# The part in front of the tile loop rebuilt in a kernel with patch attention and two window-attention layers

## What is computed

```
xn = layernorm(x)                        # x: (1, 2048, 128), float32
# patch attention on xn
qkv  = xn[:, patch_index, :] @ Wqkv.T    # 26 patches of 20 rows
attn = softmax(q @ k.T * 8**-0.5)        # 16 heads
p    = xn.at[:, patch_index, :].set(attn @ v) @ Wout.T + bout
# two layers, f = xn at first
h = shift_token(f)                       # the upper 64 channels one position later
q, k, v = split(h @ wqkv)                # q, k: normalised per head, scaled, rotated
f = f + local_attention(q, k, v) @ wo
h = layernorm(shift_token(f)); a, g = split(h @ w1 + b1)
f = f + (a * gelu(g)) @ w2 + b2
out = x + p + f
```

## Time and profile before

| what | us |
|---|---|
| median of 3 runs | 424.98 |
| lowest and highest run | 422.65, 426.35 |
| the profiled execution, whole | 424.36 |
| span of that execution, first to last instruction | 422.2 |
| PE busy in the span | 364.5 |
| DVE busy | 293.7 |
| ACT busy | 297.3 |
| POOL busy | 257.5 |

### The profile page before, as it was taken

The page is one execution under the profiler, slowest core; times in us unless marked ns, Lnnn a source line. Parts: engine busy times, 40 slices in busy tenths (PEclk is TensorE's granted clock), DMA queues, the critical chain, the costliest instruction groups (busy, mean ns, idle before and its releaser), DMA issues. The chain is left out here.

```text
span 422.2 us, 10798 instructions
## 1 busy us (share of the span) xinstructions
PE 364.5 (86%) x3999; PEld 277.9 (66%) x3999; DVE 293.7 (70%) x525; ACT 297.3 (70%) x909; POOL 257.5 (61%) x232
## 2 busy tenths in 40 slices
PE   1737855799999999998969878799999999988995
PEld 0626644578888888876636446688888888765563
DVE  4797875587787777864745766678777787565363
ACT  2334651689999898998617468889989899974621
POOL 2173589598888888892003548988888888710000
PEclk9976995899999999999989989999999999999999
DMA  8920000123232232231320003123223222110001
GB/s 294 347 77 2 2 2 2 37 53 74 50 73 61 57 71 53 63 71 33 92 121 0 0 0 77 44 55 71 57 57 73 51 68 66 46 36 12 25 25 50
DMA packets 34514, 25.80 MB, mean 61 GB/s; under 512 B 18933, under 2 KB 29087, under 8 KB 33951
## 3 DMA queue, kind: packets, MB, share of 16 engines
q1 hardware_dynamic: 34175, 24.66, 21.8%
q10 hardware_dynamic: 288, 0.46, 0.4%
HBM read 9.64 MB, written 1.05 MB: 25 GB/s over the span
## 5 line engine op out<-in xcount | busy, mean ns | idle before, releaser
L1006 ACT ACTIVATE probs<-ps,neg_max 128x128 f32<-128x128 f32 x256 | 90.1, 378 | 5.5 <-DVE neg_max L1229 4.4
L531 POOL TENSOR_TENSOR qkn<-rot 128x512 f32<-128x512 f32 x64 | 80.5, 1280 | 11.7 <-PE ps L728 4.1
L539 POOL TENSOR_TENSOR qkn<-qkn,rnorm 128x512 f32<-128x512 f32 x64 | 65.5, 1045 | 22.9 <-ACT rnorm L956 22.9
L545 POOL TENSOR_TENSOR probs_n<-probs,row_inv 128x512 f32<-128x512 f32 x64 | 66.6, 1042 | 19.1 <-DVE row_inv L1234 16.2
L1006 ACT ACTIVATION_READ_ACCUMULATOR probs<-ps,neg_max 128x1 f32 x256 | 55.4, 216 | 0.0
L949 ACT ACTIVATE sq<-ps 128x1024 f32<-128x1024 f32 x32 | 32.8, 1026 | 30.0 <-DVE rot L1181 19.2
L520 POOL TENSOR_TENSOR h_lo<-xin,h_hi 64x512 fp32r<-64x512 f32 x16 | 20.6, 1290 | 43.1 <-DVE sin_w L1189 26.9
L1229 DVE TENSOR_REDUCE neg_max<-ps 128x4 f32<-128x512 f32 x64 | 41.0, 681 | 8.3 <-PE ps L742 8.3
L173 PE MATMUL ps<-wqkv_hi,h_hi 128*128 128x512 f32 x96 | 42.8, 446 | 0.0
L1181 DVE TENSOR_TENSOR rot<-ps,cos_w 128x1024 f32<-128x1024 f32 x32 | 39.1, 1221 | 3.6 <-PE ps L175 3.0
L1171 DVE TENSOR_REDUCE ss<-sq 128x16 f32<-128x1024 f32 x32 | 38.8, 1212 | 3.9 <-ACT sq L949 3.8
(11 more groups left out here) (127 smaller groups left out, 806.1 us busy)
## 6 DMA issues: line engine op xcount, KB each, us to landing
v_off<-v_tok SPq DMA_DIRECT2D x64, 128.0 KB, 2.3
k_t<-k_t SPq DMA_DIRECT2D x30, 128.0 KB, 2.3
cos_w<-in_cos_t SPq DMA_DIRECT2D x2, 1024.0 KB, 7.9
sin_w<-in_sin_t SPq DMA_DIRECT2D x2, 1024.0 KB, 9.5
x_shift<-x SPq DMA_DIRECT2D x64, 32.0 KB, 1.9
x_raw<-in_x SPq DMA_DIRECT2D x4, 256.0 KB, 4.7
out<-o_t SPq DMA_DIRECT2D x4, 256.0 KB, 2.3
x_shift<-in_wqkv SPq DMA_DIRECT2D x1, 768.0 KB, 7.4
```

Source lines behind the costliest of these rows:

```text
L531: pool.tensor_tensor(to, first, second[:, :, ::-1, :], ALU.add).then_inc(rot_summed, 1)
L539: pool.tensor_tensor(of, of, rnorm[:, part * HEADS:(part + 1) * HEADS].unsqueeze(2) .broadcast_to([P, HEADS, DH]), ALU.mult).then_inc(rot_ ...
L545: pool.tensor_tensor(probs_n[:, 4 * g:4 * g + 4, :], probs[:, 4 * g:4 * g + 4, :], row_inv[:, 4 * g:4 * g + 4].unsqueeze(2).broadcast_to([ ...
L1006: e = act.activation(probs[:, k, :], s_ps[g][:, cw * P:(cw + 1) * P], ACT.Exp, bias=neg_max[:, k:k + 1], accum_out=row_sum[:, k:k + 1])
```

## The change

Most of it is in front of the loop.

- Patch projections: queries and keys for all blocks in two chunks of 272 columns straight from `xin` (`project_patch_qk`, `take_patch_qk`), in place of 112 columns per step. The staging on DVE is gone; POOL repeats the patches with six copies (`repeat_patches`), blocks 0 to 5, 6 to 11 and 12.
- Patch softmax: the unnormalised exponential is turned. The values get four columns of ones per group of heads (`A_VAL` = 36 in place of 32), so that the weighing gives the sums too, and DVE divides its output from PSUM (`patch_out`). The outputs of all steps are kept and turned at the end, four steps first and then three, and put with one strided copy each.
- Input: spans 2 and 3 are normalised at the end of DVE's steps 0 and 1, turned in PE's steps 2 and 3. The shifted input for the tile projection is made by two DMAs per span (`shift_input`) into `xs`, which lies in x1; ACT rounds it in one piece (`round_first`, steps 3 to 6), POOL splits it in one piece: spans 0 and 1 before the loop, spans 2 and 3 in the loop's steps 1 and 3.
- POOL's order before the loop: ones, repeats, tables, wqkv of layer 0, split of span 0, masks, split of span 1, w1. Layer 1's wqkv is rounded and split by POOL after the first layer's tiles; the unpatched positions are copied by a DMA on SP.
- Semaphores: cos, sin and the scales have one each. SP loads the scales and wqkv of layer 0 first, then cos, sin, masks. The masks arrive in `w_raw`, and `probs_t` has two buffers of its own.

Constants, SP and POOL:

```diff
+A_CHUNK = 272
+A_VAL = 36
+TURN_FIRST = 4
...
+            shift_input(0)
+            shift_input(1)
             sp.dma_start(wo_s[:], wo.rearrange("l (c p) n -> p l c n", p=P)).then_inc(w_in, 16)
...
+            shift_input(2)
+            shift_input(3)
             sp.wait_ge(xn_tr, SPANS)
             sp.dma_start(w1_raw, w1.rearrange("l p n -> p l n")).then_inc(w1_in, 16)
+            sp.wait_ge(masks_done, 1)
+            sp.dma_start(wqkv_raw[1], wqkv[1]).then_inc(wqkv_in[1], 16)
+            sp.wait_ge(a_ot_done, 2)
+            sp.dma_start(x_patch[:, PATCHED:N], xin[:, 1 + PATCHED:1 + N]).then_inc(patch_rest_done, 16)
...
+            def repeat_patches(part):
+                first, blocks = ((0, 6), (6, 6), (12, 1))[part]
+                of = xin[:, 1 + first * BLOCK:1 + (first + blocks) * BLOCK].rearrange(
+                    "p (b i s) -> p b i s", i=PATCH, s=SHIFT)
+                to = a_rep[part].rearrange("p (b s) r i -> p b s r i", s=SHIFT)
+                for s in range(SHIFT):
+                    pool.tensor_copy(to[:, :, s], of[:, :, :, s].unsqueeze(2)
+                                     .broadcast_to([P, blocks, 4, PATCH])).then_inc(a_rep_done, 1)
+            pool.wait_ge(xin0_done, 1)
+            repeat_patches(0)
+            pool.wait_ge(xin0_done, 2)
+            repeat_patches(1)
+            repeat_patches(2)
+            pool.wait_ge(scale_in, 32)
+            for table, table_in in ((cos_w, cos_in), (sin_w, sin_in)):
+                pool.wait_ge(table_in, 16)
...
             split_wqkv(0)
+            split_first(0)
+            pool.wait_ge(masks_in, 16)
+            pool.tensor_copy(masks[:], masks_f).then_inc(masks_done, 1)
+            split_first(1)
+            pool.wait_ge(w1_in, 16)
...
+                    if layer == 0 and t in (1, 3):
+                        split_first(2 + t // 2)
+                        pool.wait_ge(h_split, 3 + t // 2)
...
                 over_tiles(pool, step)
                 if layer < LAYERS - 1:
                     pool.wait_ge(rot_scaled, 2 * (n0 + TILES))
+                    pool.wait_ge(wqkv_in[layer + 1], 16)
+                    pool.tensor_copy(wqkv_hi[:, layer + 1, :], wqkv_raw[layer + 1]).then_inc(wqkv_rounded, 1)
+                    split_wqkv(layer + 1)
```

PE, one patch step and the part in front:

```diff
             def patch_step(t, parity):
                 if there(t, A_STEPS):
+                    patch_scores(t)
                 if there(t - 1, A_STEPS):
                     turn_patch_probs(t - 1)
+                if t in (2, 3):
+                    pe.wait_ge(a_v_done, t)
+                    turn_input(t)
+                    weigh_patch_values(t - 1)
+                    pe.wait_ge(xin0_done, t + 1)
+                if there(t + 1, A_STEPS) and t >= 0:
+                    project_patch_values(t + 1)
+                if t == 0:
+                    project_patch_qk(1)
+                if there(t - 1, A_STEPS) and t not in (2, 3):
+                    weigh_patch_values(t - 1)
...
                     turn_input(0)
                     pe.wait_ge(aw_in, 16)
+                    project_patch_qk(0)
+                    project_patch_values(0)
                     turn_input(1)
```

ACT, one patch step:

```diff
+                if t == 0:
+                    take_patch_qk(1)
+                if t in (2, 3):
+                    take_input(t)
+                    if t == 2:
                         act.wait_ge(wqkv_in[0], 16)
+                    round_part(0, (t - 2) * W_PART)
+                if 3 <= t < 3 + SPANS:
+                    round_first(t - 3)
```

DVE, one patch step, and what follows the steps:

```diff
+            def patch_out(t):
+                after(dve, a_op_done, t + 1)
+                inv = a_inv[:].rearrange("p (g h) -> p g h", g=4)
+                dve.reciprocal(inv, a_op[:, :, 4 * A_DH:]).then_inc(a_inv_done, 1)
+                after(dve, a_inv_done, t + 1)
+                dve.tensor_tensor(a_o[:, t, :].rearrange("p (g h d) -> p g h d", g=4, h=4),
+                                  a_op[:, :, 0:4 * A_DH].rearrange("p g (h d) -> p g h d", h=4),
+                                  inv.unsqueeze(3).broadcast_to([P, 4, 4, A_DH]), ALU.mult).then_inc(a_o_done, 1)
             def patch_step(t, parity):
+                if there(t, A_STEPS):
+                    patch_differences(t)
                 if there(t - 2, A_STEPS):
+                    patch_out(t - 2)
+                if there(t, A_STEPS):
+                    patch_values(t)
+                if t in (0, 1):
+                    normalize_input(t + 2)
...
             over_patches(dve, patch_step, in_front)
+            dve.wait_ge(tables_done, 4)
+            rotate(0, 0, cos_w)
+            rotate(0, 0, sin_w)
+            patch_out(A_STEPS - 1)
+            sum_squares(0)
+            put_patches(0)
             rotate(1, 1, cos_w)
             rotate(1, 1, sin_w)
+            put_patches(1)
             sum_squares(1)
...
-                after(dve, tab_in, 64 + 32 * layer)
+                after(dve, cos_in if table is cos_w else sin_in, 16 * (layer + 1))
```

More of the change, by code:

```diff
@@ L240, in build @@
         h_lo = sb("h_lo", [P, 1 + N], F32R)
-        sq = sb("sq", [P, 2 * INNER])
+        xs = x1
+        work = sb("work", [P, 6 * INNER])
+        rot1, rot2, sq = (work[:, 2 * INNER * i:2 * INNER * (i + 1)] for i in range(3))
         ss = sb("ss", [P, 2 * HEADS])
@@ L569, in _ @@
                         split_input(layer, g)
[L570 removed]
+                    pool.wait_ge(h_split, rounded(layer, SPANS - 3))
                     sum_rotated(n0)
@@ new lines, in put_patches @@
+            def put_patches(half):
+                after(dve, a_ot_done, half + 1)
+                first, blocks = ((0, 2 * TURN_FIRST), (2 * TURN_FIRST, PATCH_BLOCKS - 2 * TURN_FIRST))[half]
+                to = x_patch[:, first * BLOCK:(first + blocks) * BLOCK].rearrange("p (b i s) -> p b s i", i=PATCH, s=SHIFT)
+                of = a_ot[half][:, 0:blocks * 64].rearrange("p (b s i) -> p b s i", s=SHIFT, i=32)
+                dve.tensor_copy(to, of[:, :, :, 0:PATCH]).then_inc(a_out_done, 1)
```

333 lines of the change are left out of this document (140 added, 193 removed).

## The result

| | before | after |
|---|---|---|
| median, us | 425.67 (4 runs, 422.65 to 426.44) | 406.27 (4 runs, 404.10 to 407.23) |
| ratio to before | | 0.955, 95% interval 0.9488 to 0.9612 |
| the profiled execution, whole | 424.36 | 406.56 |
| its span | 422.2 | 404.8 |

The account below looks back on a forecast made before the run. PE was taken to bound the loop, the order of its chains the front. Front -18.4, loop +2.0 and end of layer 0 +1.2 sum to -15.2 us: forecast 409.5 us, likeliest case 404.5 to 413 (0.52), range 399 to 417.

Parts of the forecast that it names:

- (a): Patch steps in front of the loop: from 4.15 to 3.2 us each, or 5 us while the clock is low.
- (e): Step 2 to the first tile's rotations: steps of 6.1, 3.9, 3.2, 3.2 and 1.9 us, rotations ended at 49.7.
- (b): Head of the front, PE's first products and ACT's copies: DVE through with step 0 at 16.7 us.
- (c): POOL's new repeat copies in the front: 0.5 us per 480 elements, tables from 16.5 to 26.1 us.
- (d): DVE's scalings of spans 2 and 3 wait out POOL's table products: 8.4 us lost, DVE free at 26.2.
- Rival 1: No turns between DVE's scalings and POOL's tables: front gain 25 to 26 us, time 402 us; chance 0.20.
- (f): POOL's new order before the loop: from the rounded weight at 37.1 us, 12.3 us of work, through at 49.4.
- (g): POOL's first sum to first scores: 8.0 us plus 1.2 for hand-overs; scores at 59.0, front gain 18.4 us.
- (h): Tile loop: POOL's two extra splits cost about 1.0 us each, +2.0 us in all (bounds 0 and 2.6).
- (i): End of layer 0: POOL's weight split locks DVE, 3.4 us later, separate semaphores give part back; net +1.2.
- Rival 2: Clock stays slow through the patch steps: first scores about 67 us, front gain 10.5, time 417 us; chance 0.18.
- Rival 4: Slow steps, locks and loop costs eat the gain: 424.2 us, no change; chance 0.06.

Follow-up runs that it names:

- e4b: After, with POOL's rounding and splitting of layer 1's weight waiting until DVE has split three spans of the first feed-forward part; 405.18 us.
- e5b: After, with DVE's scaling of the cos table waiting for the sin table too, as before the change; 410.61 us.
- e2: After, with POOL's table products waiting until all input is normalised; 400.15 us (median of two executions).
- e3: After, with ACT copying the last step's turned probabilities before it squares the first tile; 406.22 us.
- e10: After, with POOL's splits of spans 2 and 3 ahead of the tile loop instead of behind tiles 1 and 3; 407.80 us.
- a0_after: The changed kernel measured once more, with no edit; 405.85 us.
- e9: After with the edits of e2 and e4b, and SP's transfers of wo, a_wout, w2 and the vectors moved behind w1's; 400.40 us.
- e8: After with the edits of both e2 and e4b; 400.97 us.
- e6b: After, with POOL's four table products cut into eight of half the size; 404.58 us (one execution).

## Why the prediction was right, and where its terms were off

The time lies in the range, on the side of the gain, and the likeliest case held. That it lies so near is in part luck: sizes that were off by 1 to 3 us had opposite signs, and a slow stretch of the clock that was not foreseen is in the sum. By its steps:

(a) and (e), the patch steps: mechanism right, size off. Late steps take 2.7 and 2.5 us where 3.2 was said, and step 2 and 3 from maximum to maximum 5.0 and 4.0 (6.1 and 3.9). The mis-sized term is the weighing, which I scaled from 0.90 to 1.0 by its columns; it is 0.47. In the old form four products in a row write the same 32 rows of the output, in the new one each writes other rows than the one before; that this is the cause was not tried. At the lower level, too, it is short: 0.71 us at 27.91. Rotations of the first tile ended at 46.6, not 49.7.

(b) right within 0.9 us: DVE was ready for the scalings at 15.80 (16.7 said). The first two products over 272 columns start 1.04 us apart (9.39 and 10.43), as said, and those of the second chunk take 0.62; it is the values of step 0 and the turn of span 1 that were quicker (1.5 and 0.6 us, with 2.0 and 1.1 said). ACT's copies took 0.40 us each, not 0.35.

(c) right: the 480-element repeats take 0.60 to 0.70 us (0.5 taken, bounds 0.46 and 1.1), and the tables run from 16.12 to 25.50 (16.5 to 26.1). Rival 3 is out.

(d) right in mechanism and in its end (DVE free at 26.35, 26.2 said), not in its distribution. Of the four scalings of span 2 one slipped in ahead of the first product and three waited; then one of span 3's waited out the last product: 6.9 us lost (9.11 - 2.24), 8.4 said. So four of eight scalings waited, not four of four. The same total falls otherwise in other runs of the same front: 5.38 + 3.69 us in e4b, 1.12 + 7.88 in e5b. In each of these runs the two engines take turns while both have such work queued. By the rule of the Trainium skill ("SBUF — State Buffer", section Who interferes with whom) alone one product's 2.4 us would be lost (an estimate); it does not say who is next when both have work queued. Rival 1 is what e2 builds by force: the first scores come 23.1 us before those of before (25 to 26 said), and the profiled execution takes 401.86 us (402 said).

(f) POOL was through with w1 at 46.17 (49.4 said), since ACT's second half of the weight was there at 34.3 and not at 37.1; the rest of its chain took 11.8 us against 12.3.

(g) The step that failed, and not only in its size: from POOL's first sum to the first scores 10.7 us, with 9.2 said (8.0 as before and 1.2 for hand-overs). The 8.0 was taken from a kernel in which POOL itself was late, so that the norms of the first tile were ready when its first sum ended (POOL's scaling follows without a wait):

```profile
71.81 2.04 POOL L539 TENSOR_TENSOR qkn<-qkn,rnorm 128x512 f32<-128x512 f32 x2
```

Now POOL's first sum follows the rotation at once, and its scaling L606 waits 2.31 us for ACT's `rnorm`. That wait is nearly all of the 2.7 us over the 8.0. It has a path: I had looked at the queues of SP and POOL, not at ACT's, where the copy for the last weighing stands behind `norms(0)`; PE idles 3.66 us for it, DVE 2.38 for PE, and DVE's sum of squares, which `rnorm` needs, stands behind that in its queue. With the copy ahead (e3) and with POOL later (e10) the scaling waits 0.70. The front did not get shorter by it in e3, where a slow stretch made the first rotation later.

The steps' 3.0 us too much and (g)'s 1.5 too little make 57.5 of the forecast's 59.0: front gain 19.9 (18.4 said).

(h) Sign right, half the size: +1.0 us, not +2.0. The tile distances with the splits are 7.71 and 8.73 us, where they were 7.50 before; the three after them are 7.49 to 7.50, where they were 7.61 to 7.62: PE did win some of it back, which I had excluded. e10 shows that it is the splits.

(i) +1.5 us (1.2 said), by the path that was said, but the nearness is luck. The cast is locked for 3.1 us (3.55 - 0.43) and the tables are issued 3.1 us later by it; a slow stretch adds 1.5 in after. With the same lock the stage takes 59.66 us in e2 and 61.84 in a0_after, that is -0.2 to +2.0 against before. The separate semaphores are worth 4.5 to 4.9 us of the stage (e5b), 2.2 to 2.4 of it by the wait alone.

Sum in the profile: -19.9 + 1.0 + 1.5 = -17.4 us.

Rival 2 (slow clock through the steps) didn't happen in after: 0.50 in 26 to 30 us, 0.61 in 30 to 34, 1.00 from 34 to 46; it is low again in the second tile's projection (0.59 in 46 to 50 us). Rival 4 falls with it. The clock also blurs what a repair is worth: the mean granted clock up to the first scores is 0.85 in after, 0.91 in e2 and e9 and 0.87 in e8, so part of their gain is less time at the lower level, whether or not the edits brought that about.

## What to carry to other kernels

Where DVE and POOL both have work from SBUF to SBUF queued, as here the scalings and the table products, reckon with one whole POOL instruction for each DVE instruction. Keep short DVE work on a critical chain away from long POOL products by an explicit wait: here that gave 3 us at the first scores, while cutting the products up or moving the DVE work ahead of other critical work gave nothing that the runs tell.

When a step is rebuilt, read the order of every engine's queue at its end, ACT's too, and don't carry an interval over from a profile in which another engine was the late one: what was ready then may be waited for now. Don't scale the row of a product by its columns when its form and order change too. One semaphore for two transfers whose first already opens a way is worth splitting: here the median is 4.3 to 4.8 us better for one line.

Before you put a stage's gain down to an edit, look where the slow stretches of the clock fall in both profiles, and whether they begin before the edit can act.

## What the runs showed of the hardware that was not expected

- PE can run out of instructions, as the count and the traffic in e9's section say. Holes of 2.79, 2.09 and 2.32 us (e2, e8, e9) with no releaser lie inside groups that share one wait; a packet (0.02 MB) of the instruction queue starts within 0.5 us of the start of each, the DMA engines are full there (share 1.02 in 22 to 26 us of e2, 1.00 in 30 to 34 us of e9), and the hole moves with that traffic. In after no such hole is seen: DVE's lock made PE idle there anyway (23.0 to 23.5 us has the packet), so a late packet would be covered there; part of what removing the lock should give is lost to the hole.
- Within the lock, cutting POOL's instructions in half halves the wait of one DVE instruction (about 1.3 in place of 2.4 us) but not the sum (8.4 and 9.1 us for eight scalings).
- The same front with the same waits can fall at either clock level in one stretch: the six products of a projection took 1.5 us in after and 2.7 in e3, though up to there the two kernels have the same instructions. At the end of layer 0, too, the same instructions ran with a slow stretch in after and a0_after and without one in e2 and e6b.
